# Sixteen attention items on one core: the weighing moved ahead of x's transposes, the softmax shifts turned earlier and placed by way of DRAM

## The reference, cut to what matters

```python
x = x + layernorm(attention(layernorm(x)))      # q, k, v with bias; two ropes on q and k
x = x + layernorm(ffn(layernorm(x)))            # gated silu, 1408 inner channels, ternary weights
# attention: scores = q k^T / 4, causal mask, softmax over the keys, times v, then Wo and bias
```

## Time and profile before

| | us |
|---|---|
| median of 3 runs | 2727.72 (2722.85 to 2729.41) |
| profiled execution, its own time | 2721.53 |
| its span, first to last instruction | 2719.8 |
| TensorE busy | 2431.0 (89%) |
| VectorE busy | 1926.6 (71%) |
| ScalarE busy | 1437.2 (53%) |
| GpSimd busy | 1161.0 (43%) |

### The profile page before, as it was taken

How to read it: one execution, slowest core, us unless ns; L and a number is a source line. 1 busy time by engine, 2 the same in 40 slices (tenths; PEclk the granted TensorE clock), 3 DMA queues, 4 the chain that set the end, 5 groups by cost and what they waited for, 6 DMA issues and landing times. The chain is left out here.

```text
span 2719.8 us, 54601 instructions
## 1 busy us (share of the span) xinstructions
PE 2431.0 (89%) x18816; PEld 1144.8 (42%) x18816; DVE 1926.6 (71%) x5887; ACT 1437.2 (53%) x1902; POOL 1161.0 (43%) x1531
## 2 busy tenths in 40 slices
PE   4889999999999999999999974199999999999997
PEld 2434444443444443444444331044444444444443
DVE  5878888888888888888888871745555555555554
ACT  3567777776767776777777662422222222222221
POOL 4566776776776776676777653000000000000000
PEclk8999999999999999999999997599999999999999
DMA  4344545544544554554453432301111111111111
GB/s 164 117 132 131 167 132 156 166 140 142 171 148 141 160 158 132 170 160 140 153 167 117 154 120 98 163 16 47 66 57 46 47 61 46 57 67 46 46 46 47
DMA packets 178934, 305.62 MB, mean 112 GB/s; under 512 B 32416, under 2 KB 115872, under 8 KB 165536
## 3 DMA queue, kind: packets, MB, share of 16 engines
q1 hardware_dynamic: 178720, 302.86, 34.4%
HBM read 182.73 MB, written 119.01 MB: 111 GB/s over the span
## 5 line engine op out<-in xcount | busy, mean ns | idle before, releaser
L752 DVE CUSTOM_DVE_ANT_0 mx<-mx,causal 128x512 f32<-128x512 f32 (+3 forms) x2048 | 944.8, 519 | 156.1 <-PE mx L863 155.9
L586 ACT ACTIVATE probs<-ts,exp_scale 128x1024 f32<-128x1024 f32 x640 | 708.7, 1107 | 165.0 <-PE ts L877 163.2
L1152 ACT ACTIVATE silu<-gu,gate_scale 128x512 f32<-128x512 f32 x176 | 120.9, 687 | 631.2 <-PE gu L1343 631.2
L1127 POOL TENSOR_TENSOR f_rstd<-f_var,f_neg_half 128x4 f32<-128x4 f32 x32 | 32.3, 1009 | 928.7 <-DVE f_var L1270 646.0
L1293 DVE SCALAR_TENSOR_TENSOR hidden<-gu,up_scale,silu 128x512 f32<-128x512 f32 x176 | 131.9, 750 | 416.3 <-PE gu L1343 406.3
L464 POOL TENSOR_SCALAR_AFFINE_SELECT probs<-probs 128x512 f32<-128x512 f32 x512 | 339.1, 681 | 57.6 <-ACT probs L586 56.4
L891 PE MATMUL xb<-probs,vs 128*32 128x512 f32 (+3 forms) x4096 | 308.5, 442 | 56.7 <-ACT shift_rows L592 29.0
L1341 PE MATMUL gu<-f_xT_hi,gate_hi 128*128 128x512 f16 x704 | 267.9, 381 | 52.4 <-issue 52.4
L752 DVE DVE_READ_ACCUMULATOR2_ANT row_max<- 128x1 f32 x2048 | 286.8, 140 | 0.0
L877 PE MATMUL ts<-qT,kT 64*128 64x512 f16 (+3 forms) x2048 | 246.1, 298 | 28.3 <-ACT probs L586 28.2
L1343 PE MATMUL gu<-f_xT_lo,gate_hi 128*128 128x512 f16 x704 | 267.9, 381 | 0.0
(11 more groups left out here) (145 smaller groups left out, 4367.9 us busy)
## 6 DMA issues: line engine op xcount, KB each, us to landing
slots<-half SPq DMA_DIRECT2D x260, 128.0 KB, 13.6
qT<-slots SPq DMA_DIRECT2D x128, 256.0 KB, 3.7
kT<-slots SPq DMA_DIRECT2D x128, 256.0 KB, 3.8
weighed<-oT SPq DMA_DIRECT2D x128, 256.0 KB, 4.9
xn<-x SPq DMA_DIRECT2D x16, 1024.0 KB, 7.6
xr<-x SPq DMA_DIRECT2D x16, 1024.0 KB, 7.6
slots<-half SPq DMA_DIRECT2D x256, 64.0 KB
spread<-recips SPq DMA_DIRECT2D x64, 256.0 KB
```

The source lines that it names most:

```text
L586: nc.scalar.activation(probs[:, g % 2, u, :, :], ts[:, :, :], ACT.Exp, scale=exp_scale[:, 0:1]).then_inc(ts_read, 1)
L752: last = nc.vector.tensor_tensor_reduce(out=scores, in0=scores, in1=causal[:, T - P * (qt + 1):T], scale=1.0, scalar=-3e38, op0=ALU.add, o ...
```

## The change

The work of each item stays the same but for the shifts. Five edits:

1. TensorE turns the shifts of a group with one transpose in place of four. For that, `row_max`, `row_shift` and `shift` are laid out with the query tile as the last dimension, and `shift_rows` has 32 partitions of 128 numbers in place of 8 of 512.
2. `turn_shift` stands ahead of the q/k projection in u = 1, that is, ahead of its second half; on ACT `read_shift` stands ahead of `add_bias`.
3. SP writes the turned rows to a DRAM tensor `shifts` (`send_shift`, u = 2), and reads them back into the four partitions of `qT` (`place_shift`), at u = 3 behind `fetch_slots`.
4. TensorE weighs ahead of x's transposes. `BANK_USES` now gives the weighing the bank of the shifts in every group, and x the bank of the q/k projection. ACT's `read_weighed` stands ahead of `high_of_x`.
5. DVE's `low_of_x` moves from u = 3 to u = 4.

```diff
             BANK_USES += [(("qk",) + QUERIES_KEYS[g], r), (("s", (g + 1) % NG, (g + 1) // NG), 1 - r),
+                          (("av", (g - 1) % NG, (g - 1) // NG), 1 - r)]
             if TURNED[g]:
-                BANK_USES.append((TURNED[g], 1 - r))
+                BANK_USES.append((TURNED[g], r))
                 r = 1 - r
-            BANK_USES += [(("av", (g - 1) % NG, (g - 1) // NG), 1 - r), (V_OR_OUT[g], r)]
+            BANK_USES.append((V_OR_OUT[g], r))
...
             def place_shift(i, g):
-                turned_rows, placed = held(sp, NG * i + g + 1), held(sp, 32 * (NG * i + g))
+                pairs = slice(2 * (g % 2), 2 * (g % 2) + 2)
+                sp.wait_ge(shift_out, 16 * (NG * i + g + 1))
+                sp.dma_start(qT[SHIFT_ROWS, g // 2, pairs, :],
+                             shifts[g % 2].rearrange("(p r t) k -> r p (t k)", p=2, t=NT)).then_inc(shift_in, 16)
+
+            def send_shift(i, g):
+                turned_rows, placed = held(sp, NG * i + g + 1), held(sp, 16 * (NG * i + g))
                 sp.wait_ge(shift_read, turned_rows)
                 wait_if_any(sp, shift_in, placed)
-                for pair in range(2):
-                    sp.dma_start(qT[SHIFT_ROWS, g // 2, 2 * (g % 2) + pair, :],
-                                 shift_rows[4 * pair:4 * pair + 4, g % 2, :]).then_inc(shift_in, 16)
+                sp.dma_start(shifts[g % 2], shift_rows[:, g % 2, :]).then_inc(shift_out, 16)
...
                     if u == 2 and exists(i + (g + 1) // NG):
-                        place_shift(i + (g + 1) // NG, (g + 1) % NG)
+                        send_shift(i + (g + 1) // NG, (g + 1) % NG)
                     if u == 3 and exists(i + owner):
                         fetch_slots(i + owner, n)
+                    if u == 3 and exists(i + (g + 1) // NG):
+                        place_shift(i + (g + 1) // NG, (g + 1) % NG)
...
-                nc.scalar.activation(shift_rows[0:8, g % 2, :], xb16[0:8, bank_of("s", g), 0:T], ACT.Copy).then_inc(shift_read, 1)
+                nc.scalar.activation(shift_rows[:, g % 2, :], xb16[0:8 * NT, bank_of("s", g), 0:P], ACT.Copy).then_inc(shift_read, 1)
...
                     if u == 2:
+                        if exists(i + (g + 1) // NG):
+                            read_shift(i + (g + 1) // NG, (g + 1) % NG)
                         if exists(i + owner):
                             add_bias(i + owner, n)
-                        if exists(i + (g + 1) // NG):
-                            read_shift(i + (g + 1) // NG, (g + 1) % NG)
...
                     if u == 3:
+                        if exists(i + (g - 1) // NG):
+                            read_weighed(i + (g - 1) // NG, (g - 1) % NG)
                         if TURNED[g]:
                             kind, c, of = TURNED[g]
                             if in_turn(kind, i + of):
                                 high_of_x(i + of, c, bank_of(kind, c))
-                        if exists(i + (g - 1) // NG):
-                            read_weighed(i + (g - 1) // NG, (g - 1) % NG)
...
-                    if u == 3 and TURNED[g]:
+                    if u == 4 and TURNED[g]:
                         kind, c, owner = TURNED[g]
                         if in_turn(kind, i + owner):
                             low_of_x(i + owner, c, bank_of(kind, c))
...
-                for t in range(NT):
-                    last = nc.tensor.transpose(xb16[0:8, bank, P * t:P * (t + 1)],
-                                               shift[:, t, :, :, :].rearrange("p j a l -> p (j a l)"), ident16[:, :])
-                last.then_inc(shift_full, 1)
+                nc.tensor.transpose(xb16[0:8 * NT, bank, 0:P], shift[:, :, :, :, :].rearrange("p j a l t -> p (j a l t)"),
+                                    ident16[:, :]).then_inc(shift_full, 1)
...
+                    if u == 1 and exists(i + (g + 1) // NG):
+                        turn_shift(i + (g + 1) // NG, (g + 1) % NG)
                     if u < 2 and exists(i + owner):
                         project_queries_keys(i, n, owner, u)
-                    if u == 1 and exists(i + (g + 1) // NG):
-                        turn_shift(i + (g + 1) // NG, (g + 1) % NG)
                     if u == 2:
+                        if exists(i + (g - 1) // NG):
+                            weigh(i + (g - 1) // NG, (g - 1) % NG)
                         if TURNED[g]:
                             kind, c, owner = TURNED[g]
                             if in_turn(kind, i + owner):
                                 wait_for_bank(pe, i, kind, c)
                                 turn_x(i + owner, c, bank_of(kind, c))
-                        if exists(i + (g - 1) // NG):
-                            weigh(i + (g - 1) // NG, (g - 1) % NG)
```

More of the change, by code:

```diff
@@ L68, in power_of_two_scales, with attention_phase @@
     link(nc.vector.tensor_scalar(unscale, power, 0.25, None, ALU.mult))
-def attention_phase(nc, x, wT, bias_row, bias_columns, rope_cos, rope_sin, slots, weighed, recips, x1):
+def attention_phase(nc, x, wT, bias_row, bias_columns, rope_cos, rope_sin, slots, weighed, recips, shifts, x1):
     ctx = ExitStack()
@@ L119, in attention_phase @@
             "p (n c o) -> p n c o", n=4, c=NC)
[L120 to L123, removed]
+        row_max = sb("row_max", [P, 2, 2, 2, NT])
+        row_shift = sb("row_shift", [P, 2, 2, NT])
+        shift = sb("shift", [P, 2, 2, 2, NT], F16)
+        shift_rows = sb("shift_rows", [8 * NT, 2, P], F16)
         oT = sb("oT", [P, T])
@@ L186, in attention_phase @@
         shift_read = sem("shift_read")
+        shift_out = sem("shift_out")
         shift_in = sem("shift_in")
@@ L250, in attention_phase @@
         for g in range(NG):
-            BANK_USES += [(("qk",) + QUERIES_KEYS[g], r), (("s", (g + 1) % NG, (g + 1) // NG), 1 - r)]
+            BANK_USES += [(("qk",) + QUERIES_KEYS[g], r), (("s", (g + 1) % NG, (g + 1) // NG), 1 - r),
+                          (("av", (g - 1) % NG, (g - 1) // NG), 1 - r)]
             if TURNED[g]:
-                BANK_USES.append((TURNED[g], 1 - r))
+                BANK_USES.append((TURNED[g], r))
                 r = 1 - r
-            BANK_USES += [(("av", (g - 1) % NG, (g - 1) // NG), 1 - r), (V_OR_OUT[g], r)]
+            BANK_USES.append((V_OR_OUT[g], r))
             r = 1 - r
@@ L471, in shift_of_maxima @@
                 wait_if_any(pool, shift_full, NG * i + g)
-                nc.gpsimd.tensor_scalar(shift[:, :, :, :, 0], row_max[:, g % 2, :, :, :], -1.0 / SHIFT_UNIT, None,
+                nc.gpsimd.tensor_scalar(shift[:, :, :, 0, :], row_max[:, g % 2, :, :, :], -1.0 / SHIFT_UNIT, None,
                                         ALU.mult).then_inc(shift_step, 1)
@@ L476, in shift_of_maxima @@
                 pool.wait_ge(shift_step, 2 * (NG * i + g + 1))
-                nc.gpsimd.tensor_tensor(shift[:, :, :, :, 1], row_shift[:, :, :, :], shift[:, :, :, :, 0],
+                nc.gpsimd.tensor_tensor(shift[:, :, :, 1, :], row_shift[:, :, :, :], shift[:, :, :, 0, :],
                                         ALU.subtract).then_inc(shift_ready, 1)
@@ L589, in read_shift @@
             def read_shift(i, g):
-                wait_if_any(act, shift_in, 32 * (NG * i + g - 1))
+                wait_if_any(act, shift_out, 16 * (NG * i + g - 1))
                 act.wait_ge(shift_full, NG * i + g + 1)
-                nc.scalar.activation(shift_rows[0:8, g % 2, :], xb16[0:8, bank_of("s", g), 0:T], ACT.Copy).then_inc(shift_read, 1)
+                nc.scalar.activation(shift_rows[:, g % 2, :], xb16[0:8 * NT, bank_of("s", g), 0:P], ACT.Copy).then_inc(shift_read, 1)
             def read_weighed(i, g):
@@ L753, in maxima @@
                             out=scores, in0=scores, in1=causal[:, T - P * (qt + 1):T], scale=1.0, scalar=-3e38,
-                            op0=ALU.add, op1=ALU.max, accum_out=row_max[:, g % 2, qt, pair, j:j + 1])
+                            op0=ALU.add, op1=ALU.max, accum_out=row_max[:, g % 2, pair, j, qt:qt + 1])
                 last.then_inc(mx_read, 1)
@@ L871, in transposed_scores @@
                 if u == 0:
-                    pe.wait_ge(shift_in, 32 * (NG * i + g + 1))
+                    pe.wait_ge(shift_in, 16 * (NG * i + g + 1))
                 wait_if_any(pe, ts_read, NS * i + n)
@@ L1449 @@
     recips = nc.dram_tensor("recips", (NC, P, 8 * T // P), F32, kind="Internal").ap()
+    shifts = nc.dram_tensor("shifts", (2, 8 * NT, P), F16, kind="Internal").ap()
     attention_phase(nc, ap["x"], [ap[f"w{n}T"] for n in "qkvo"], ap["bo"], ap["bias_columns"],
-                    ap["rope_cos"], ap["rope_sin"], slots, weighed, recips, x1)
+                    ap["rope_cos"], ap["rope_sin"], slots, weighed, recips, shifts, x1)
     ffn_phase(nc, x1, ap["gateT"], ap["upT"], ap["downT"], ap["gate_s"], ap["up_s"], ap["down_s"], out)
```

## The result

The changed kernel is slower by 0.8%: 2743.78 us median of 5 runs (2740.0 to 2761.45) against 2724.73 (2720.11 to 2729.41) for the kernel before; the ratio is 1.008, 95% interval 1.006 to 1.0099. The forecast was 2678 us and faster. The profiled execution took 2740.08 us, with a span of 2738.4, 18.6 more than before.

The account below looks back on a forecast made before the run. TensorE was taken to set the pace, busy 927.5 of 1000 us. A gain of 7.7 less 5.0 of placement waits gave 2.7 us an item, 43 in 16 items, so 2721.5 became 2678 us; range 2610 to 2750.

Parts of the forecast that it names:

- One transpose for four: TensorE's shift transposes: three fewer save 0.24 us a group, 1.9 an item; the 32 columns cost nothing.
- Turned and read earlier, weighing first: TensorE's unit 2 bank waits go, but about 0.4 us in group 4; the shift read takes 0.17 us.
- What TensorE gains: TensorE, per item: 7.1 us idle plus 1.9 of transposes, less 0.4, 0.3 and 0.6 that stay: 7.7.
- What the DRAM pass costs: TensorE's waits at ts for the placement, landing at F + 4.5: 5.0 us an item, between 0.7 and 14.5.
- F: Start of the slot fetch (fetch_slots) on SP, in us; the placement was taken to land at F + 4.5.
- Rival B: SP's round trip of write, fetch and placement becomes the bound: at F + 6.0 45 us slower, 2766; chance 0.20.
- A: The placement lands in time: at F + 3.5 only group 3 is late, by 1.5 us, 2622 us; chance 0.25.
- C: TensorE's bank wait for ACT's shift read stays, 4 of 7.1 us an item: 2721 us; chance 0.08.

Follow-up runs that it names:

- e2_direct: Kernel before with the changed order alone (shifts turned and read earlier, weighing first, low_of_x later), four transposes and direct placement at unit 2 kept: 2684.81 us.
- k2_filler: Changed kernel with six extra matmuls on TensorE ahead of the wait for the placement in groups 3 and 4: 2751.0 us.
- e1_place_first: Changed kernel with the placement ahead of fetch_slots on SP, not behind it: 2733.21 us, ratio 1.0043.
- h1: f1 with GpSimd's averaging moved behind its turning of q or k, ScalarE's and VectorE's readers a step later: 2681.45 us, ratio 0.9834.
- f1: e2_direct with the averaging's reads moved ahead of fetch_slots on SP in even groups: 2681.62 us, ratio 0.9841.
- m4_weighed_into_gap: e1_place_first with the averaging's reads moved ahead of both fetch_slots and the placement on SP: 2924.45 us, ratio 1.0744.

## Why the prediction was wrong

By its own steps, in us an item:

- *One transpose for four*: forecast 1.9, measured 1.3 (0.16 a group). I divided the 0.32 us of the four by four. In the trace of before the last of them starts 0.17 behind the first (811.96), so they follow each other at 0.06, and the next matmul starts 0.15 behind the last. Three fewer save 3 x 0.06; that the 32 columns cost next to nothing, as I took, is right.

```profile
812.13 0.22 PE L901 MATMUL xb<-ident,shift 128*8 128x128 f16 x1
812.28 0.34 PE L863 MATMUL mx<-kT,qT 64*128 64x384 f16 x2
```

- *Turned and read earlier, weighing first*: right in the changed kernel, where 3.9 of 64.3 us are left per 1000. The shift read takes 0.25 us on the mean and not the estimated 0.17.
- *What TensorE gains*, 7.7: too high. I let 1.3 of the old waits stay; where the placement does not hold TensorE, in e2_direct, others come up and the sum is 4.4. In the changed kernel only 1.0 an item of waits other than the placement's shows, so there this miss is hidden behind the placement's wait.
- *What the DRAM pass costs*, 5.0: the mechanism was right and the size too small. The landing at F + 4.5 was F + 4.8, and F itself came 0.2 to 0.8 later, since the slot writes did not land within the 2.0 us that I took: at 813.76 it is 2.03 behind the last issue's end, but 2.2 to 2.8 on the mean of the groups that I had given 2.0. The waits sum to 65.8 x 0.0996 = 6.6. Their order is the forecast one: from 500 to 1500 us they are longest in total behind group 3 (15.7 us) and all but gone behind group 4 (1.6).
- *The clock*: missing. I priced a wait as its own length, at a clock that stays at 1.00. With the dips each item lost another 1.9, against 0.2 before. In the changed kernel's own rows this is the step that failed most: the waits went up by 0.4 (7.6 against 7.1), the transposes down by 1.3, the clock cost 1.7 more, together +0.8 of the measured +0.9. The forecast had -0.8, -1.9 and 0. This is a reckoning and no experiment. At full clock TensorE would be at `ts` earlier and wait longer there, and k2_filler raised the clock without a gain in time, so that the clock alone turned the sign is not shown.
- *The two halves*, as the experiments split them. For edits 2, 4 and 5 without the one transpose the forecast's terms give 7.7 - 1.9 = 5.8 an item, 93 us; e2_direct gained 40. For the pass with the one transpose they give 5.0 - 1.9 = 3.1, 50 us; from e2_direct to the changed kernel it is 59, the dips counted in. So of the 62 us by which the forecast was off, 53 lie in *What TensorE gains*: even with a placement in time and a clock of 1.00 the new order gives less than the pass takes.
- Rival B, slower, came true at F + 4.8, below the point I gave it, F + 5.3: that point sets the waits against a gain of 7.7 and has no clock in it. Its price of 45 us was for F + 6.0; measured are 19.
- A, the placement in time, is excluded for the changed kernel by 76 such waits in the whole run; C by the 3.9 us left of L899's.

The Trainium skill's rule (*DMA: Bandwidth & Descriptors*, Queues, rings and completion order) is that a DMA's count cannot come before the earlier writes of the engines that it runs on. The trace agrees: 3.4 us behind the fetch, 1.6 alone. My forecast read the rule as "not before the fetch's count", which is more than it says: it holds engine by engine.

The standstill of SP, which neither it nor my sum had, is no step of this forecast. In the changed kernel SP waits 3.8 us per 1000 for the send, and GpSimd's wait for the averaged tile is what it was:

```profile
POOL averaged L491 <- DMA averaged<-weighed: 92.0, 39, 4.9
```

Before it was 95.7. The standstill decides what comes of the obvious repair: when the placement goes ahead of the fetch, as in e1_place_first, the first wait goes and the second stands.

By this reckoning the item of the steady stretch is accounted for to within 0.1 us. That is 14 of the 19 us; the other 5 lie outside the stretch and were not looked into. What is left open is which of ScalarE, GpSimd and VectorE's loads sets e2_direct's 45.8 us. The fastest version here, h1 at 2681.45 with f1 and e2 within its interval, keeps the new order and drops the DRAM pass: 1.7% faster than before.

## What to carry to other kernels

A transfer moved behind another on an in-order queue is late by the whole chain ahead of it, and a wait on such a queue is paid by everything behind it; follow both to their last reader before you price the transfer itself. When a change takes out one engine's waits, look in the same timeline for who was just in time: here the new order was worth 40 us, and 0.16 us of transposes a group was bought with a pass through DRAM that costs more. And count what a wait of a microsecond or two on TensorE does to its clock behind it: here the dips cost 1.9 us an item on top of 7.6 of waits.

## What the hardware showed that I had not expected

At idle stretches of TensorE of 1.7 to 3.3 us, in a stretch otherwise at full clock, the granted clock of the changed kernel fell to 0.50 for 3.4 us, though the engine was busy again for all or most of it: 1.7 us lost each time. Length alone does not tell: of the waits over 1.6 us from 500 to 1100 us in the changed kernel, those of 1.64, 1.89, 1.92 and 2.51 us had no dip behind them, that of 1.72 had one, and the kernel before had one at 1.35. With many long waits the mean fell further, to 0.94 in m4_weighed_into_gap. An 8 KB write to DRAM took 2.0 us to land on the median (1.3 to 4.8), and in e1_place_first SP waited 5.2 us from its issue at 817.44, some 6.6 us after a 1 MB store had been issued.
